# A fused cross-attention, self-attention and mixture-of-experts kernel: one phase transition, the routing of the last tiles and the closing chain in another order

## What is computed

```python
x = x + cross_attention(layernorm(x), ctx_768)   # 32 x 32 rows of 512 ; 257 context keys of 384, one head
x = x + self_attention(layernorm(x))             # 16 heads of 32, rotary embedding, 32 rows a sequence
x = x + experts(layernorm(x))                    # 8 experts 512 -> 1024 -> 512, best 2 of each row

def experts(xf):                                 # 1024 rows
    scores = sigmoid(xf @ gate_w.T + balance_bias)
    top, idx = top_k(scores, 2)                  # weights top / (sum + 1e-6)
    h = silu(einsum('td,ehd->teh', xf, w1))
    return sum over the two experts of weight * (h @ w2.T)
```

## Time and profile before

| | |
|---|---|
| median of 3 runs | 543.81 us (542.87 to 544.47) |
| the profiled execution | 544.36 us, its span (first to last instruction) 542.4 us |
| busy share of the span: PE, DVE, ACT, Pool | 90%, 70%, 47%, 21% |
| mean granted clock of TensorE | 0.962 of full speed |
| HBM read, written | 75.82 MB, 29.43 MB |

### The profile page before, as it was taken

How to read it: one execution, slowest core, us unless ns; L and a number is a source line. 1 busy time by engine, 2 the same in 40 slices (tenths; PEclk the granted TensorE clock), 3 DMA queues, 4 the chain that set the end, 5 groups by cost and what they waited for, 6 DMA issues and landing times.

```text
span 542.4 us, 11280 instructions
## 1 busy us (share of the span) xinstructions
PE 489.0 (90%) x3722; PEld 281.0 (52%) x3723; DVE 378.4 (70%) x847; ACT 255.4 (47%) x397; POOL 113.3 (21%) x86
## 2 busy tenths in 40 slices
PE   3997999998988999975769899999999999999992
PEld 1743455555666676755555444445444454444541
DVE  3778897848979899898886877663746637673230
ACT  1313446555168385765642745544625445552220
POOL 0022212015050231300663022111121111221111
PEclk9999799999999999996968999999999999999997
DMA  8999578910009996166852589994895848743333
GB/s 296 406 398 366 174 292 325 407 49 1 1 1 351 381 381 228 40 232 211 293 201 83 152 268 256 287 246 126 226 241 141 248 112 233 232 75 61 58 58 40
DMA packets 55201, 110.95 MB, mean 205 GB/s; under 512 B 24416, under 2 KB 25600, under 8 KB 50048
## 3 DMA queue, kind: packets, MB, share of 16 engines
q1 hardware_dynamic: 25296, 87.80, 44.7%
q10 hardware_dynamic: 25568, 12.94, 10.1%
q0 software_dynamic: 4304, 9.77, 8.4%
HBM read 75.82 MB, written 29.43 MB: 194 GB/s over the span
## 4 chain that ended last, share of the span: by engine, by line
PE 64%; DVE 20%; DMA 5%; issue 3%; ACT 3%; SPq 2%; POOL 2%; DVEq 0%; ACTq 0%; POOLq 0%
PE bank L768 18%; PE bank L786 18%; PE bank L555 6%; PE bank L371 4%; DMA ctx_region<-in_ctx 4%; PE bank L539 3%; DVE wbuf L1590 2%; PE bank L520 2%; PE bank L581 2%; PE bank L469 2%; PE bank L750 1%; DVE small L1144 1%; DVE ctx_region L1387 1%; PE bank L515 1%; DVE small L1141 1%
## 5 line engine op out<-in xcount | busy, mean ns | idle before, releaser
L768 PE MATMUL bank<-wbuf,ctx_region 128*128 x480 | 108.2, 382 | 0.0
L1590 DVE SCALAR_TENSOR_TENSOR wbuf<-ctx_region,wbuf 128x2048 f32 (+1 forms) x28 | 62.9, 2288 | 30.4 <-ACT wbuf L953 29.0
L1821 POOL DMA_INDIRECT out<-misc,ints x21 | 39.7, 1892 | 205.1 <-ACT misc L1034 146.4
L768 PEld LDWEIGHTS bank<-wbuf,ctx_region 128*128 128x128 f16 x480 | 46.5, 99 | 53.0 <-issue 1.8
L953 ACT ACTIVATE wbuf<-ctx_region 128x2048 f32 (+1 forms) x28 | 52.0, 1904 | 27.8 <-issue 21.2
L1724 POOL TENSOR_TENSOR small<-small 128x2 f32<-128x2 f32 (+2 forms) x25 | 27.3, 1096 | 164.3 <-DVE small L1117 161.5
L786 PE MATMUL bank<-wbuf,actT 128*128 x264 | 58.8, 379 | 1.0 <-DVE actT L1681 1.0
L1053 ACT ACTIVATE ctxT_region<-bank 128x512 f32<-128x512 f32 x42 | 25.0, 597 | 69.2 <-PE bank L768 55.7
L786 PE MATMUL bank<-wbuf,xn 128*128 x240 | 53.4, 379 | 0.0
L555 PE MATMUL bank<-ctx_region,wbuf 128*128 128x256 f16 x384 | 43.3, 273 | 3.7 <-DVE ctx_region L1272 3.7
L786 PEld LDWEIGHTS bank<-wbuf,actT 128*128 128x128 f16 x264 | 25.8, 98 | 32.0 <-issue 1.2
(11 more groups left out here) (222 smaller groups left out, 800.0 us busy)
## 6 DMA issues: line engine op xcount, KB each, us to landing
ctx_region<-in_experts SPq DMA_DIRECT2D x28, 1024.0 KB
routed_rows<-ctxT_region SPq DMA_DIRECT2D x1, 16900.0 KB, 50.7
ctxT_region<-in_ctxT SPq DMA_DIRECT2D x8, 1542.0 KB, 11.8
ctx_region<-in_ctx SPq DMA_DIRECT2D x8, 1536.0 KB, 8.9
ctx_region<-routed_rows ACTq DMA_DIRECT2D x21, 260.0 KB, 3.2
wbuf<-in_experts SPq DMA_DIRECT2D x4, 1024.0 KB
out<-x ACTq DMA_DIRECT2D x8, 256.0 KB
wbuf<-in_wqT SPq DMA_DIRECT2D x4, 256.0 KB, 5.3
```

What stands on the lines that cost most here:

```text
L768: mm = nc.tensor.matmul(bank[half][:, :], xgT[:, b, x_part, k * P:(k + 1) * P], w16[:, ds(at + (w_part + k * EH + half * 512), 512)], star ...
L1590: nc.vector.scalar_tensor_tensor(w16[:, ds(at + (LOW + n * PIECE), PIECE)], src_[:, piece], W_SCALE, w16[:, ds(at + (HIGH + n * PIECE), PI ...
L1821: nc.gpsimd.indirect_dma_start(out, bass.IndirectOffsetOnAxis(idx[:, slot_no:slot_no + 1].bitcast(U32), axis=0), y_out[:, slot_no, :], Non ...
```

## The change

1. *Transition.* `xnT` gets a second home in `shared` for pairs 1 and 3. SP issues the loads of `swq` and `swk` in pair 1 instead of pair 2. ACT cuts the high half of weights 0, 1, 2 in pairs 1, 2, 3; DVE cuts the low halves of 0 and 1 at the end of pair 2's part, behind a wait for Pool's last context root, and the third behind `first_scale(1)`. In the last pair DVE instead of ACT centres the context sums. `normalised_out(1)` comes before `values_out(0)` on ACT. On DVE the last context residual, the fourth cut, `turn_cos`, `normalised_low(1)` and `turn_sin` are interleaved. Pool's two memsets come later: `k_exp` after the third low cut, `p_T` after the keys are rotated.
2. *Pairs.* On DVE `first_scale` sits between `turn_cos` and `turn_sin`; in pair 0 `attended_low` and `normalised_low` come before `turn_cos` of the next queries.
3. *Routing of the last tiles.* Pool scatters one row set, then `features_low`, then one more before its root, and the rest after it. `mark(0)` is split around the second half of the statistics. On PE two tiles of `first_rows` go behind the transposes, and the last two tiles are collected high part first. On DVE `choose_gates(1)`, `slots_out(1)` and the first `cut_low` go behind the last rows' low half. On ACT the cut of piece 3 goes behind the copy of the first tile's rows.
4. *First product.* It no longer waits for `rt_slots`; the loops over channel blocks and halves are exchanged.
5. *Closing chain.* The last tile's second product is made in two halves of 256 columns in two banks, ACT scales each as it comes; ACT, not Pool, waits for the last landing; `finished` is incremented by both.

```diff
+        xnT_homes = (xnT, shared[:, 4 * ROW:4 * ROW + KC * 2 * P].bitcast(F16).rearrange("p (a k t) -> p a k t", a=2, k=KC))
...
-                if pair == 2:
+                if pair == 1:
                     sp.wait_ge(s["qkb_ps"], 1)
                     load_w(swq, "swqT", s["self_qk_in"])
                     load_w(swk, "swkT", s["self_qk_in"])
...
-            sp.wait_ge(s["finished"], 1)
+            sp.wait_ge(s["finished"], 2)
...
-            first_rows(0, range(0, ROUTED[0][1]))
+            first_rows(0, range(0, 2))
             features_T(PAIRS - 1)
+            first_rows(0, range(2, ROUTED[0][1]))
...
-            first_rows(0, range(*ROUTED[2]))
+            for part in range(2):
+                first_rows(0, range(*ROUTED[2]), (part,))
...
-                pe.wait_ge(s["rt_slots"], len(ROUTED))
                 pe.wait_ge(s["xgT0"], 1)
...
-            second_product(last, 0, experts_of(last)[0])
+            pe.wait_ge(s["hT0"], last + 1)
+            pe.wait_ge(s["hT1"], last + 1)
+            for half in range(2):
+                for k in range(HC):
+                    for h_part, w_part in ((0, HIGH), (0, LOW), (1, HIGH)):
+                        column = w_part + W2_AT + k * D + half * (D // 2)
...
+                mm.then_inc(s["y2_ps"], 1)
```

```diff
@@ scalar
-                if pair + 1 == PAIRS:
-                    cut_self_high(0)
+                if pair:
+                    cut_self_high(pair - 1)
...
             turned_out(0)
-            biased(k_T, 4, s["sk_ps"], 0, "sbk", s["sk"])
-            values_out(0)
-            normalised_out(1)
             act.wait_ge(s["sw_lo"], 3)
             cut_self_high(3)
-            act.wait_ge(s["ptx_zero"], 2)
+            biased(k_T, 4, s["sk_ps"], 0, "sbk", s["sk"])
+            normalised_out(1)
+            values_out(0)
+            act.wait_ge(s["ptx_zero"], 1)
...
-            gated(last, 0)
+            act.wait_ge(s["gate"], last + 1)
+            act.wait_ge(s["added"], last + 1)
+            for half in range(2):
+                act.wait_ge(s["y2_ps"], last + (half + 1))
...
+            act.wait_ge(s["scat"], last * 16 + 16)
+            act.sem_inc(s["finished"], 1)
```

```diff
@@ vector
+                if pair + 2 == PAIRS:
+                    dve.wait_ge(s["cx_rstd"], TILES)
+                    cut_self_low(0)
+                    cut_self_low(1)
...
-            first_norm(0)
-            cut_self_low(0)
+            first_stats(0)
+            first_scale(0)
+            last_sums_centred(0)
+            first_stats(1)
+            last_sums_centred(1)
             normalised_low(0)
             sums_low(PAIRS - 1)
             dve.wait_ge(s["xnT_ps"], 2)
-            first_norm(1)
-            cut_self_low(1)
+            first_scale(1)
...
             turn(0, 0)
+            context_residual(PAIRS - 1)
             join(0, 0)
-            turn(0, 1)
+            cut_self_low(3)
+            turn_cos(0, 1)
             normalised_low(1)
+            turn_sin(1)
             join(0, 1)
-            cut_self_low(3)
...
-            choose_gates(1)
             logits_out(PAIRS - 1)
             choose_rank(2)
-            slots_out(1)
             last_features_low(0)
             place(2)
-            mark(2)
+            mark_at(2)
+            mark(range(*ROUTED[2]))
             last_features_low(1)
-            cut_low(expert0, 2 * EXPERT, (0,), 0)
+            choose_gates(1)
+            slots_out(1)
             choose_experts(2)
             choose_scores(2)
             choose_gates(2)
             slots_out(2)
+            cut_low(expert0, 2 * EXPERT, (0,), 0)
@@ gpsimd
             pool.wait_ge(s["cv_ps"], TILES)
+            pool.wait_ge(s["sw_lo"], 3)
             nc.gpsimd.memset(k_exp, 0.0).then_inc(s["ptx_zero"], 1)
...
-                    scatter(0, first_to_store[0:2])
+                    scatter(0, first_to_store[0:1])
                     features_low(pair - 1)
-                    scatter(0, first_to_store[2:3])
+                    scatter(0, first_to_store[1:2])
...
-            pool.wait_ge(s["scat"], last * 16 + 16)
```

109 lines of the change are left out of this document (63 added, 46 removed).

## The result

The changed kernel took 539.29 us (median of 8 runs, 537.58 to 547.28) where the kernel before, on the same chip and beside it, took 543.61. The ratio is 0.9919 with an interval of 0.9899 to 0.994. Forecast were 532.1 us and a range of 530.0 to 537.0: the sign was right, the gain was 4.3 us instead of 11.7, and the time lies outside the range. In a later set of five runs the same kernel took 534.84 us, ratio 0.9827 (0.9801 to 0.9854), inside the range. Single executions can stand far off (547.28 us here, at a mean granted clock of 0.926 where the others had 0.963 to 0.972; 1747.3 us once in pool_waits, unexplained): they are in the medians and ranges given here, but not in the ratios.

A forecast was written before the change was run, and what follows sets the result against it. PE, busy 90% of the span, was taken as the bound, with gains only where it stands still. Gains of 4.0 (A + B), 4.7 (C) and 3.0 (D) sum to 11.7, giving a median of 532.1 us, range 530.0 to 537.0.

The forecast's parts named there:

- A: Transition: second home for `xnT`, weight cuts earlier, memsets later, centring on DVE; scores(0) gain 2.95 us (bounds 2.3 and 3.3).
- the rival in which it holds the turn: Transition: the turn is held or `k_exp` comes late, A + B is 1.0, 535.1 us; chance 0.08.
- the slow landing: ACT's queue: the cut of `swq` waits for its DMA; at 28 us landing 546 us; chance 0.04.
- B: Pairs: reordered DVE work shrinks its waits and starts the later softmaxes earlier; gain 1.05 us (bounds 0 and 1.4).
- C: Routing tail and first expert product; gain 4.7 us (bounds 3.0 and 6.0).
- C.1: Routing tail: two marks move behind the statistics, last normalisation starts 1.7 us earlier (bounds 0.8 and 1.7).
- C.2: Last logits: first_rows(2, 3) on PE ahead of them costs 0.95 us; ready at 272.2, 1.75 us earlier.
- C.3: First product no longer waits for the slots, DVE's idle 4.09 us goes; cut_hidden(0) starts 5.0 us earlier.
- C.5: ACT's wait for 16 scatters: last starts at 289.5, lands in time but for 0.5 us; cover 1.3 us.
- C.4: PE idles 3.4 us before tile 1, so product 2 loses 0.3 us more to the clock (bounds 0 and 1.3).
- scatters late: Rival: all eight scatters take 1.90 plus 0.3, fields come 5.2 us late, 537.3 us; chance 0.10.
- D: Program end: Pool's DRAIN of 3.09 us runs beside the last landing; gain 3.0 us (bounds 0 and 3.1).

The follow-up runs named there:

- pool_waits: The changed kernel with Pool again waiting for the landing of the last row scatter, ACT waiting too; 540.2 us, ratio 0.9944.
- closing_alone: The kernel before with the edits of the closing chain alone; 541.81 us, ratio 0.9964.
- tail_alone: The kernel before with the edits of the routing tail and the first product alone; 544.54 us, ratio 1.0023.
- after_again: The changed kernel once more without an edit, in a later set; 534.84 us, ratio 0.9827.
- product_waits: The changed kernel with the first expert product's wait for the last slots given back; 539.17 us, ratio 0.9926.

## Why the prediction was too low, step by step

**A, right.** Forecast 2.95, measured 3.1 (from the last scores of the cross attention to softmax(0), 45.14 to 42.09); the other 0.6 of the lead of 3.67 stems from before 115 us. PE had no stop at 150. The profile of before is a base on the low side here: the same distance is about 46.8 us in closing_alone and 46.6 in tail_alone, which have the old transition too, and 42.1 in all seventeen profiles with the new one. In both a group of 48 matmuls ran for some 3 us at a granted 0.50 (130 to 133 and 154 to 157) and took 7.08 us instead of 5.42. Timelines of PE of closing_alone and tail_alone:

```profile
129.71 7.08 PE L555 MATMUL bank<-ctx_region,wbuf 128*128 128x256 f16 x48 [1.25 <-DVE ctx_region L1291]
```

```profile
152.66 7.08 PE L555 MATMUL bank<-ctx_region,wbuf 128*128 128x256 f16 x48 [2.49 <-DVE ctx_region L1270]
```

So A gave 3.1 us against one profile of the old order and about 4.6 against the two others; no term of the forecast had this.

The first memset ran from 133.17 to 136.68 beside a shuffle of DVE (135.36) that took 1.34 us, its length in the other pairs too (1.29 to 1.36); the rival in which it holds the turn is out. The cut of `swq` cost nothing at 78 us, and the slow landing, the rival on the slower side, did not come.

**B, nearly right.** Forecast 1.05, measured 0.9. That "pair 2 is unchanged" failed in this profile by 1.2 us, by a stretch at the low clock that code without the change can have too.

**C, the step that failed.** Forecast 4.7. By its terms, for the two profiles of the changed kernel against that of before:

| term | forecast | after | after_again |
|---|---|---|---|
| C.1, softmax(3) to the last normalisation, 22.15 us before | 1.7 | 1.0 | 1.0 |
| C.2, from there to the last logits, 5.30 | 0.05 | -2.15 | 0.9 |
| C.3, to the cut of the hidden values, 18.68 | 3.25 | 3.1 | 2.4 |
| C.5 (no wait for the scatters), to PE's second half of tile 1, 17.12 | 0 | -1.9 | -0.9 |
| C.4 (the clock), the loop to the last tile | -0.3 | 0.6 | 0.6 |
| sum | 4.7 | 0.7 | 4.0 |

*C.1* gave its 1.7 at the marks: from the first residual of the last pair to the second DVE took 2.59 us instead of 4.29. But 0.6 was lost ahead of them, where DVE now waits 0.93 us for PE's output product (258.92 in after).

*C.2* carries the largest error. The 3.2 us of the earlier trace rows were taken as the price of the logits and the modelled records of PE as its time; that a result can come 3 us after the modelled end was in no term and in no rival.

*C.3* held to 0.2 us in after: DVE did from the logits to the hidden values what the replay said. But product_waits shows that it was the order on DVE and not the product's freed wait.

*C.5* assumed 17.1 us of DVE without a wait, by a cover of 1.3 us. It was used up: the slots of tiles 4 and 5 came at 277.71 where the replay of the forecast has 278.0 less the lead of 4.0, thus 274.0; the logits alone are 3.6 us late (271.75 for 268.2). With the late logits and slots put back behind the rest, the last scatter left at 290.38 instead of 285.5 (289.5 less the lead), and DVE waited 1.83 us. ACT's load leaves 2.76 us behind the start of the last scatter in after and in after_again (290.38 to 293.14, 286.53 to 289.29). In after a second thing would have held it as long: ACT's copy of the rows ahead of the load started at 291.96, 3.3 us behind the modelled end of PE's 48 matmuls, another late result, and ended at 293.03; in after_again it started at 286.23, in time. Even in after_again 0.56 us of DVE's wait are left.

That was the rival "scatters late", only that its mechanism, eight longer scatters, was not the one: six of the eight took 0.96 to 1.26 us, and they started too late. Had I followed Pool's queue instead of its sum, the idle time in the middle (6.41 us, 3.38 in after_again) would have been seen. Against tails without a slow second tile (mean 276.8) C is worth 2.3 at its best: the forecast took the one disturbed profile of before as its base.

The two marks under the root did no harm: they ran at 263.33 for 0.61 us, the root at 263.51 for 0.75, and DVE waited 0.37 for it. As the prediction applied it, the rule of the Trainium skill (SBUF — State Buffer, "SBUF: two separate sides") on the exclusive lock of the shared ports would have had the marks hold the root; these rows don't show it. The rule speaks of DVE instructions with two SBUF inputs or in a two-port mode, and nothing here shows that these marks are either. The two-input instruction of the marks, which had taken 1.69 us beside Pool's cut, took 0.15 at 260.26, 0.3 us after Pool's cut had ended. That agrees with the rule.

**D, right in kind, wrong in size.** Forecast 3.0, measured 1.8 (8.2 to 6.4) from the start of the last scatter to the end of the span. I had read from the earlier trace rows that the DRAIN of 3.09 us is a time of its own. It is so only in its first part; some 1.5 us come behind the landing.

**The sum.** In the profiles: 0.6 less at softmax(3) (3.36 for 4.0), 4.0 less in C, 0.9 less behind the last tile, which makes the 5.6 us between the forecast's 11.7 and the 6.1 of the spans. For after_again the same sum is 3.9, 4.0 and 2.0, together 9.9 for 11.7. That its time lies inside the range is owed to the width of the range and to luck: D was still 1.0 us short, and C reached even its 4.0 only against the tail with the slow second tile. One figure of the prediction was also added up wrongly: PE at tile 1 "near 296.0 (309.77 - 4.0 - 5.0)" is 300.8 by its own terms; it was at 306.33, and at 302.47 in after_again. The range had left out what failed: each term was bounded by its rows, and none by the chance that PE's records say less than the semaphores.

## What to carry to other kernels

Read when a result reaches the engine that waits for it, not when the matmul's record ends: among many small matmuls the two were up to 4 us apart here. When work is moved within one engine, follow every queue that its result feeds, instruction by instruction, for idle time in the middle; a queue with the same sum can end later. Take the base of a replay from more than one profile where the clock can fall, and measure a change with two times on more than one set of runs.

## What the runs showed of the hardware

- Results of PE (logits, counts, rows of the first tile) reached their waiting engine up to 4.2 us after the modelled end, in eight of the fifteen profiles with edits of C and in none of the five without, among many small matmuls; two executions of one kernel differ in it (4.4 and 7.45 us for the logits), at the same granted clock in the records.
- Pool's DRAIN at the end of the program takes 3.09 us when all DMAs have landed, and 5.09 to 5.56 us, to some 1.5 us behind the landing, when a scatter is open. Leaving the landing to another engine hides half of it.
- Stretches at a granted 0.50 fall at the same place in some executions of the same code and not in others: 1.2 us more in the 28.4 between two softmaxes, 1.66 us more in a group of 48 matmuls of 5.42.
- A Pool memset of 3.51 us did not hold a DVE shuffle beside it (1.34 us), and two one-input normalisations that had taken 4.16 us beside a memset took 0.99 without one.
